# A product-key retrieval layer: from dense products for every tile of tokens to fetched rows for three tiles in four

## The reference

```python
q = (hidden_states @ w_queries.T).reshape(b, t, 2, h, n)
sim = jnp.einsum('btphn,hkpn->pbthk', q, keys)
sx, ix = jax.lax.top_k(sim[0], k)
sy, iy = jax.lax.top_k(sim[1], k)
all_scores = (sx[..., :, None] + sy[..., None, :]).reshape(b, t, h, k * k)
all_idx = (ix[..., :, None] * nk + iy[..., None, :]).reshape(b, t, h, k * k)
scores, pos = jax.lax.top_k(all_scores, k)
indices = jnp.take_along_axis(all_idx, pos, axis=-1)
de = down_embed[indices]
ue = up_embed[indices]
ew = jnp.einsum('btd,bthkd->bthk', hidden_states, de)
ew = jax.nn.silu(ew) * jax.nn.softmax(scores, axis=-1)
experts_states = jnp.einsum('bthk,bthkd->btd', ew, ue)
mlp = jax.nn.silu(hidden_states @ w_gate.T) * (hidden_states @ w_up.T) @ w_down.T
return mlp + experts_states
```

## Time and profile before

| what | us |
| --- | --- |
| median of 3 runs (10445.38 to 10500.5) | 10450.3 |
| the profiled execution, its own time | 10466.0 |
| its span, first to last instruction | 10464.2 |
| mean granted clock of TensorE, share of full speed | 0.892 |

### The profile page before, as it was taken

How to read it: one execution, slowest core, us unless ns; L and a number is a source line. 1 busy time by engine, 2 the same in 40 slices (tenths; PEclk the granted TensorE clock), 3 DMA queues, 4 the chain that set the end, 5 groups by cost and what they waited for, 6 DMA issues and landing times. The chain is left out here.

```text
span 10464.2 us, 134852 instructions
## 1 busy us (share of the span) xinstructions
PE 8774.6 (84%) x51394; PEld 5200.4 (50%) x51506; DVE 5572.0 (53%) x9096; ACT 4189.2 (40%) x6715; POOL 2222.1 (21%) x2590
## 2 busy tenths in 40 slices
PE   4888583985898979999996988889886999999999
PEld 1222242652333346646643544444343444799998
DVE  6777441014776736526634887765544666343343
ACT  3666230111555546415622676652221444222221
POOL 1010112011111001101100443330000110566665
PEclk8888675985999989999997998989886999999999
DMA  3222142111222100000000000000001322100000
GB/s 67 41 41 41 36 66 78 65 57 39 41 41 41 24 22 1 4 13 7 1 4 14 1 1 1 1 3 8 6 1 29 58 45 44 44 1 1 1 1 17
DMA packets 161954, 263.21 MB, mean 25 GB/s; under 512 B 38699, under 2 KB 78485, under 8 KB 159543
## 3 DMA queue, kind: packets, MB, share of 16 engines
q1 hardware_dynamic: 155175, 240.91, 11.4%
q0 software_dynamic: 6144, 13.64, 0.4%
HBM read 165.30 MB, written 75.53 MB: 23 GB/s over the span
## 5 line engine op out<-in xcount | busy, mean ns | idle before, releaser
L819 ACT ACTIVATE probs<-scores 128x1024 f32<-128x1024 f32 (+4 forms) x960 | 868.4, 937 | 873.6 <-PE scores L696 618.4
L908 DVE TENSOR_REDUCE row_max<-ring 128x1 f32<-128x512 f32 (+3 forms) x1792 | 1025.4, 628 | 238.5 <-PE ring L670 213.5
L696 PE MATMUL scores<-query_stack,key_stack 99*128 99x512 bf16 (+3 forms) x2816 | 846.2, 391 | 164.4 <-DVE levels L930 77.8
L716 PE MATMUL outputs<-probs,head_values 128*32 128x512 f32 (+3 forms) x5632 | 778.5, 627 | 101.3 <-ACT probs L816 98.6
L3950 POOL TENSOR_SCALAR r_second_hot<-constants,r_picks_t 128x128 f32<-128x128 f32 x1024 | 662.2, 664 | 431.2 <-DVE r_picks_t L4027 431.2
L816 ACT ACTIVATE probs<-levels,quant 128x1024 f32<-128x1024 uint8 x512 | 612.7, 1233 | 330.3 <-DVE levels L930 327.0
L930 DVE TENSOR_SCALAR levels<-scores 128x1024 uint8<-128x1024 f32 x512 | 607.7, 1220 | 181.4 <-PE scores L696 149.3
L670 PE MATMUL ring<-key_stack,query_stack 96*128 96x512 bf16 (+3 forms) x1792 | 607.9, 382 | 62.5 <-DMA key_stack<-normed_parts 39.9
L696 PEld LDWEIGHTS scores<-query_stack,key_stack 99*128 99x128 bf16 x2816 | 256.6, 103 | 684.6 <-DVE levels L930 278.6
L3676 DVE TENSOR_TENSOR_SCAN ssm_pre<-ssm_pre,added 128x1024 f32<-128x1024 f32 x256 | 571.0, 2271 | 33.2 <-ACT ssm_pre L3634 33.2
L3891 ACT ACTIVATE r_active<-r_psum_dots 128x512 f32<-128x512 f32 x256 | 152.7, 597 | 999.4 <-PE r_psum_dots L3811 995.3
(11 more groups left out here) (657 smaller groups left out, 16553.3 us busy)
## 6 DMA issues: line engine op xcount, KB each, us to landing
joined_heads<-heads_out SPq DMA_DIRECT2D x512, 32.0 KB, 2.0
expert_w<-in_L_ffn_w SPq DMA_DIRECT2D x16, 1024.0 KB, 11.5
quant_parts<-parts SPq DMA_DIRECT2D x48, 256.0 KB, 5.2
query_stack<-quant_parts SPq DMA_DIRECT2D x48, 256.0 KB, 8.6
key_stack<-quant_parts SPq DMA_DIRECT2D x48, 256.0 KB, 8.4
query_stack<-cross_parts SPq DMA_DIRECT2D x48, 256.0 KB, 8.2
normed_parts<-parts SPq DMA_DIRECT2D x48, 256.0 KB, 4.8
query_stack<-normed_parts SPq DMA_DIRECT2D x48, 256.0 KB, 8.6
```

The costliest lines, as they stand in the source:

```text
L696: last = nc.tensor.matmul(out[:, off:GROUP], keys, q_stack[0:rows, h, half * GROUP + off:(half + 1) * GROUP], start=True, stop=not edge)
L716: last = nc.tensor.matmul(o_ps[SLOT * i:SLOT * (i + 1), half % out_banks, off:GROUP], vals, probs[0:k_rows, n % 2, i // 2, i % 2, off:GROU ...
L819: nc.scalar.activation(dst, s_ps[0:k_rows, 2 * (e % 2):2 * (e % 2) + 2, off:GROUP], ACT.Exp, scale=scale).then_inc(probs_ready, 1)
L908: nc.vector.reduce_max(row_max[:, i, qt, at:at + 1], src[:, 0:cols], AX.X).then_inc(ring_read, 1)
```

## The change

Tiles go in groups of four: three are *fetched*, the fourth is *dense*. A dense tile is computed as before, with lanes of 8 tokens in four batches, `second_hot` made by DVE in one instruction, one buffer each of `active` and the one-hot rows, and one bank for dots. A fetched tile takes its 32 rows per token from a table in HBM that holds a down row and an up row side by side (2 KB), 16384 rows of them, so that no index needs a limit. For each of the 32 picks POOL issues one gather of 128 rows into a ring of 16 (`got`); DVE multiplies and sums it with the token's features (**dot**); per eight rows, a *beat*, ACT applies silu (**live**), DVE multiplies with the softmax weight (**weigh**), ACT spreads each weight on a diagonal matrix (**diagonal**), and TensorE adds row times diagonal into the tile's sum in two products (**mix**). The features come row-wise from a transposition on TensorE (**rows**). What decode did is DVE's now (**places**, **codes**, **picked**).

The list of steps (`retrieval_events`) has beats of eight places, twelve beats to a group. In beat k DVE computes dots of rows 8k to 8k + 7; in beat k + 1 come live, weigh and the diagonals (places 1 to 4), and the mixes at places 4 to 7. POOL has its own loop: each four gathers wait until the rows that lay there were mixed. The former mix of one-hot rows is called **weave**, the multiplication with it **blend**. SP loads the MLP's weights ahead of `down`. The first norm covers three tiles, the last covers one, the others four.

The diff, cut to its core:

```diff
--- before.py
+++ after.py
...
-LANES = SLOT // 2
+LANES = 8
 CHUNKS = 8
-BATCHES = 4
...
+BATCHES = SLOT // LANES
+PER_CHUNK = BLOCKS // CHUNKS
+FETCHED = PER_HALF - 1
+FETCHED_TILES = GROUPS * FETCHED
+GOT_ROWS = 16
+RELEASE = 4
+CYCLE = FETCHED * RHEADS
...
+            s = CYCLE * g + FETCHED * (r - 2)
+            put(s - 2, 5, "project", t)
+            put(s - 2, 7, "queries", t)
+            put(s - 1, 3, "sims", t)
+            put(s - 1, 5, "sims_copy", t)
+            for n in range(RHEADS * SIDES):
+                put(s + n // 4, 2 * (n % 4) + 1, "keys", t, n)
+            for n in range(RHEADS):
+                put(s + 2, 2 * n, "pairs", t, n)
+            put(s + 2, 7, "shift", t)
+            put(s + 3, 0, "places", t)
+            put(s + 3, 2, "exp", t)
+            put(s + 3, 3, "codes", t)
+            put(s + 3, 6, "picked", t)
+            put(s + 4, 3, "weights", t)
...
+            put(first - 3, 5, "gate", i, r)
+            put(first - 3, 6, "gated", i, r)
+            put(first - 2, 0, "multiplied", i, r)
+            put(first - 1, 5, "hide", i, r)
+            put(first - 2, 5, "rows", i)
+            put(first - 2, 7, "rows_copy", i)
+            put(first + RHEADS + 1, 2, "add", i, r)
...
+            put(CYCLE * g + 1 + j, 6, "dots", g, j)
+            put(CYCLE * g + 1 + j, 7, "silu", g, j)
+            put(CYCLE * (g + 1) + 1 + j, 5, "out", g, j)
+        put(CYCLE * g + 7, 4, "turn", g)
+        for n in range(BATCHES):
+            put(CYCLE * g + 8 + n, 7, "lanes", g, n)
+            put(CYCLE * g + 9 + n, 5, "weave", g, n)
+            put(CYCLE * g + 10 + n, 3, "blend", g, n)
...
+        put(CYCLE * g + 11, 7, "gate", g, FETCHED)
+        put(CYCLE * g + 12, 0, "gated", g, FETCHED)
+        put(CYCLE * g + 12, 2, "multiplied", g, FETCHED)
+        put(CYCLE * g + 12, 5, "hide", g, FETCHED)
+        put(CYCLE * g + 21, 6, "add", g, FETCHED)
...
+        for beat, place, kind in ((0, 6, "mean"), (1, 0, "centre"), (1, 1, "squares"), (1, 6, "var"), (1, 7, "root"), (2, 2, "inverse"), (2, 4, "spread"), (2, 7, "scale")):
+            put(at + beat, place, kind, g)
...
+        for h in range(RHEADS):
+            k = RHEADS * i + h
+            for n in range(TOP):
+                plan.setdefault((k, n), []).insert(0, ("dot", k, n))
+            plan.setdefault((k + 1, 0), []).append(("live", k))
+            plan.setdefault((k + 1, 1), []).insert(0, ("weigh", k))
+            for n in range(TOP):
+                put(k + 1, 1 + n // 2, "diagonal", k, n)
+                put(k + 1, 4 + n // 2, "mix", k, n)
+    return [event for place in sorted(plan) for event in plan[place]]
...
-        active = sb("r_active", [P, 2, BLOCKS, P])
-        second_hot, first_hot = sb("r_second_hot", [P, 2, LANES, KEYS]), sb("r_first_hot", [P, 2, LANES, 2 * BLOCKS])
+        got = sb("r_got", [P, GOT_ROWS, 2 * DIM])
+        active = sb("r_active", [P, BLOCKS, P])
+        second_hot, first_hot = sb("r_second_hot", [P, LANES, KEYS]), sb("r_first_hot", [P, LANES, 2 * BLOCKS])
+        diagonal = sb("r_diagonal", [P, TOP, P])
...
+            @block.gpsimd
+            def _(pool):
+                for i in range(FETCHED_TILES):
+                    pool.wait_ge(decoded, searched[fetched_tile(i)] + 1)
+                    for n in range(PICKS):
+                        k = PICKS * i + n
+                        if k >= GOT_ROWS and n % RELEASE == 0:
+                            pool.wait_ge(summed, k - GOT_ROWS + RELEASE)
+                        nc.gpsimd.indirect_dma_start(out=got[:, k % GOT_ROWS, :], out_offset=None, in_=io["L3_ffn_tables"],
+                                                     in_offset=bass.IndirectOffsetOnAxis(ap=index[:, i % FETCHED, n:n + 1], axis=0)).then_inc(arrived[k % GOT_ROWS], 16)
...
+                    elif kind == "rows":
+                        out = free_bank("rows", *which)
+                        for c in range(FC):
+                            last = nc.tensor.transpose(out[:, c * P:(c + 1) * P], x(fetched_tile(which[0]), c), chip.c(C_ID))
+                        last.then_inc(ring_ready, 1)
...
+                    elif kind == "mix":
+                        k, n = which
+                        i = k // RHEADS
+                        pe.wait_ge(diagonal_ready, TOP * k + n + 1)
+                        for c in range(FC):
+                            last = nc.tensor.matmul(y_of(i, 0)[:, c * P:(c + 1) * P], got[:, (TOP * k + n) % GOT_ROWS, DIM + c * P:DIM + (c + 1) * P], diagonal[:, n, :],
+                                                    start=False, stop=(k % RHEADS == RHEADS - 1 and n == TOP - 1), skip_group_check=True)
+                        last.then_inc(summed, 1)
...
+                            pe.wait_ge(dots_active, k)
...
+                    elif kind == "weave":
+                        g, n = which
+                        k = BATCHES * g + n
+                        pe.wait_ge(lanes_ready, k + 1)
                         if k:
-                            pe.wait_ge(mixed, k)
-                        for q in range(LANES // 2):
-                            lane = n % 2 * LANES // 2 + q
+                            pe.wait_ge(blended, k)
...
+                    elif kind == "live":
+                        k = which[0]
+                        act.wait_ge(dot_ready, TOP * (k + 1))
+                        nc.scalar.activation(act_w[:, k % 2, :], dot[:, k % 2, :], ACT.Silu).then_inc(live_ready, 1)
+                    elif kind == "diagonal":
+                        k, n = which
+                        if n == 0:
+                            act.wait_ge(weighted, k + 1)
+                        if k:
+                            act.wait_ge(summed, TOP * (k - 1) + n + 1)
+                        nc.scalar.activation(diagonal[:, n, :], chip.c(C_ID), ACT.Copy, scale=act_w[:, k % 2, n:n + 1]).then_inc(diagonal_ready, 1)
...
+                    if kind == "dot":
+                        k, n = which
+                        at, i = TOP * k + n, k // RHEADS
+                        if at % PICKS == 0:
+                            dve.wait_ge(*read_of("rows", i))
+                        if n == 0 and k >= 2:
+                            dve.wait_ge(diagonal_ready, TOP * (k - 1))
+                        dve.wait_ge(arrived[at % GOT_ROWS], 16 * (at // GOT_ROWS + 1))
+                        if at >= 2:
+                            dve.wait_ge(dot_ready, at - 1)
+                        nc.vector.tensor_tensor_reduce(scratch[:, at % 2, :], got[:, at % GOT_ROWS, 0:DIM], rows[:, i % 2, :], 1.0, 0.0, ALU.mult, ALU.add,
+                                                       dot[:, k % 2, n:n + 1]).then_inc(dot_ready, 1)
+                    elif kind == "weigh":
+                        k = which[0]
+                        dve.wait_ge(live_ready, k + 1)
+                        own = act_w[:, k % 2, :]
+                        tt(own, own, share[:, k // RHEADS % 2, k % RHEADS, :], ALU.mult).then_inc(weighted, 1)
...
+                    elif kind == "picked":
+                        t = which[0]
+                        flat = lambda s: code[:, s, :, :].rearrange("p h k -> p (h k)")
+                        if t % PER_HALF == FETCHED:
+                            then(ts(far[:, :], flat(0), BLOCKS - 0.5, KEYS - 1.0, ALU.is_gt, ALU.mult))
+                            then(ts(picks[:, 0, :], flat(0), BLOCKS - 1.0, None, ALU.min))
+                            then(tt(picks[:, 1, :], flat(1), far[:, :], ALU.max))
+                        else:
+                            then(stt(out=flat(0), in0=flat(0), scalar=float(KEYS), in1=flat(1), op0=ALU.mult, op1=ALU.add))
...
+                        first = first_hot[:, :, :]
+                        made(tt(second_hot[:, :, :], chip.c(C_IOTA).rearrange("p (o n) -> p o n", o=1).to_broadcast((P, LANES, KEYS)), lanes(1, KEYS), ALU.is_equal))
+                        then(tt(first, chip.c(C_PAIRED, 2 * BLOCKS).rearrange("p (o n) -> p o n", o=1).to_broadcast((P, LANES, 2 * BLOCKS)), lanes(0, 2 * BLOCKS), ALU.is_equal))
+                        tt(first, first, lanes(2, 2 * BLOCKS), ALU.mult).then_inc(lanes_ready, 1)
...
+    tables = np.concatenate([a["L3_ffn_down_embed"], a["L3_ffn_up_embed"]], axis=1)
+    io["L3_ffn_tables"] = np.pad(tables, ((0, KEYS * KEYS - EMBEDS), (0, 0)), mode="edge")
```

419 lines of the change are left out of this document (222 added, 197 removed).

## The result

The changed kernel takes 10496.8 us (median of 20 runs, 10477.0 to 10544.9) where the kernel before takes 10472.7 beside it: ratio 1.003, 95% interval 1.0017 to 1.0042. That is no change by the 0.5% bound, 24 us on the slow side, and 222 us above the forecast of 10275.

What follows compares the result with a forecast made beforehand. TensorE's work bounds the last layer (1499.7 us). Start 18, 96 beats x 13.3 = 1277, last mixes 6, last dense out 14.3 and norm 9 make 1324; forecast 10275 us, range 10000 to 10480.

Steps and rivals of the forecast that it cites:

- TensorE's, POOL's and the DVE's lists: Each engine's work per beat in the changed layer: TensorE 9.8 us, POOL 10.0, DVE 8.7.
- the rival that said so: POOL's gathers cost by their bytes: pitch 2.2 us instead of 1.25, 10690 us in all; chance 0.08.
- The dot: DVE's product and sum of 256 elements per fetched row: 0.40 us each, 3.2 us a beat.
- the path itself: From one weigh to the next, through diagonal, mixes, place 5, gather landing and dot: 13.3 us a beat with the clock.
- place 5 with its waits: TensorE's queued products between mixes 1 and 2: 3.8 us a beat, plus 0.9 for waits on blend, bank and inverse.
- beats that POOL or DVE bind: Light beats can't be under POOL's 10.0 us, and DVE is longer where lanes fall: 0.5 us a beat.
- the clock's term: TensorE's granted clock falls from 1.00 to 0.88 in the layer, adding 0.8 us a beat.
- the landing: Second gather landed, before its dot: 1.25 for the step, 2.6 to land, 0.4 for the second KB.
- The last-but-one: The ring lets nothing overlap: landing 4.5 us or dot 0.83, beats 14.9 to 15.6 us, 10420 to 10490; chance 0.09.
- The last: TensorE's clock at its lower level for most of the layer: 16.4 us a beat, 10570 us; chance 0.04.
- The collision rival: Every POOL gather waits out a DVE dot: pitch 1.65 us, beats of 14.3 us, 10370 us; chance 0.12.

Runs made afterwards that it cites:

- kept-rows run: All gathers but the first 16 left out of the changed kernel, so nobody waits for a landing: 9998.5 us beside 10486.5.
- both edits: Changed kernel with the ring released by two rows instead of four and weaves at place 7 instead of 5: 10195.8 us on chip B, 10341.2 on D.

## Why the prediction was wrong

**Right.** TensorE's, POOL's and the DVE's lists (9.7, 10.0 and 7.6 us a beat for 9.8, 10.0 and 8.7). POOL's step of 1.25 us for 2 KB rows as for 1 KB: 0.95 busy and 0.30 between, so a gather is not priced by its bytes, and the rival that said so fell. The dot: 0.42 and 0.08, next start 0.35 later, for 0.40. Diagonals 388 ns, as the earlier trace rows. No collision of gathers with the DVE in their lengths (0.99 us mean for 0.95). And the path itself, which closes piece by piece in the changed kernel's trace (means of 91 beats, to the start of what is named where nothing else is said); releasing by twos and moving the weave, which cut into it, gained 157 and 91 us.

| piece of the path | predicted, us | measured, us |
| --- | --- | --- |
| weigh, to the end of the first diagonal | 0.6 | 0.6 |
| from there to the end of mix 1 | 0.9 | 1.8 |
| from there to mix 2: place 5 with its waits | 3.8 + 0.9 | 5.6 (4.9 of work, 0.7 of waits) |
| mixes 2 and 3, to the first gather | 1.05 | 1.8 |
| first gather to the second row's dot | 4.25 | 5.3 |
| that dot to the next weigh | 0.5 | 0.4 |
| beats that POOL or DVE bind | 0.5 | in the rows above |
| the clock | 0.8 | in the rows above |
| sum | 13.3 | 15.5 |

On chips C and D the same kernel gives 15.35 and 15.36.

**Wrong, first step: the clock's term.** "I take 0.88. It acts on 5.6 us of the path: +0.8." TensorE's three pieces are 9.2 us, where the prediction has 6.65 at full clock, 0.8 for the clock and 0.5 for other beats: 1.3 us too little. The 0.88 is an average over a stretch, and the path needs the clock where TensorE works on it. That was 0.69 up to the end of mix 1 and through place 5, and 0.97 to 0.99 from the first gather to the dots, when TensorE has little to do. The products of place 5 take 4.94 us a beat at 0.69, and 3.47 in the kept-rows run at 0.98: 1.5 us in this piece alone. With 0.69 in its own sum the prediction would have had 2.5 us for 0.8. The waits inside place 5 were no larger than predicted (0.7 for 0.9). That a better clock alone would have saved this time isn't shown: the run that raised it did so with added work.

**Wrong, second step: the landing.** "The second gather landed, 1.25 + 2.6 + 0.4" measured 5.3 us for 4.25. From issue to landing it is 3.7 us (median of 261 gathers in the trace of both edits on B) for the 3.0 of the sum. The 2.6 was read where the DMA engines fall idle in the earlier trace rows; the landing of those 1 KB gathers as the trace of that later run names it is 2.9. The Trainium skill's fit for a POOL DMA (DMA: Bandwidth & Descriptors, "Anatomy of one DMA — SWDGE (gpsimd) path") gives 2.6 us for 256 KB, an estimate, which is 1.1 below the 3.7.

The two steps make up the 2.2 us a beat, and 96 x 2.2 is 211 of the 222 us. They also hang together: it is after the wait for rows that TensorE works at the lower clock.

**A term that it had at nothing: late increments.** Everything on the path was priced as if gathers in flight left the other engines' signals alone. In the rows of gathers TensorE stood still; its next product in the kernel before is

```profile
2321.28 0.69 PE L2585 MATMUL norm_psum<-constants,mixed 128*128 128x128 f32 x2 [31.08 <-DVE mixed L2576]
```

so no row could show what a gather does beside it. In the changed kernel the term is small: 1 silu of 64 and 2 releases of 89 late, and all of TensorE's waits inside place 5 are 0.7 us. In other orders it is large: 447 us between chips D and B for mixes in the first half with gathers that nobody waits for, 145 us for both edits. What the changed kernel takes on chip B stays open, since it was never run there.

**The rivals.** None was right. The last-but-one (the ring lets nothing overlap, 10420 to 10490) came closest in time, its upper end 7 us under the measurement; its landing of 4.5 us is longer than the 3.7 measured, and the clock made up the rest. The last (the lower clock for most of the layer, 10570) was wrong for the layer's mean of 0.82 to 0.84 and near for the stretches on the path. The collision rival looked for the price in POOL and DVE instruction lengths, where it isn't.

**The best version found** releases the ring by ones or twos and has the weaves at place 7: 10330 to 10341 us, ratio 0.986 to 0.987 on two chips, and by twos 0.973 on chip B. Both are faster than either kernel.

## What to carry to other kernels

Price a path with the clock of the stretches in which the path runs on TensorE, not with the mean of the layer: here 0.69 against 0.83. Then close the sum: measure each piece of the predicted path over many beats before looking for a further cause. Here the pieces add up to the beat, and what looked like the cause in other runs (late increments) has little room in this one.

To see what a wait costs, letting the transfers run with nobody waiting and then taking them away gives two differences (122 and 390 us), but they are differences between kernels: another loss can come in where the first goes out. Check it by the same count in each version. And run the unaltered kernel on every chip on which a variant is judged: the same program differed by 145 us between two chips on which the kernel before took 10486.5 and 10484.2.

## What was not expected of the hardware

- TensorE's semaphore increments came 2 to 4 us late when three gathers had been issued by POOL in the 3.5 us before, on four chips of five in most orders, and never on the fifth; the kernel before ran alike on all (10459.8 to 10486.5 us). It goes with the number of gathers (1 KB: 4.29 us, 2 KB: 3.90). ACT's and the DVE's hand-overs to each other were in time. What holds TensorE's increments isn't shown, nor whether the recording, which loses records in the same traces, has a part in it.
- The granted clock was 1.00 while TensorE stood waiting for rows and 0.50 in the 6.9 us of work after it.
- Products added to TensorE's waits raised its mean granted clock from 0.82 to 0.92 without any gain in time.
- A gather of 128 rows took POOL's 1.25 us a step for 1 KB and for 2 KB rows alike; its landing took 2.9 us for 1 KB and 3.7 for 2 KB.
- Two inputs of 256 elements, product and sum in one instruction, cost the DVE 0.42 us and a read of the accumulator of 0.08.
